# An expert layer over 63 tiles of gathered (token, expert) rows instead of 40 weight blocks over all tokens

## What is computed

```python
logits = x2d @ gate_w.T                                  # x2d: layer-normed tokens, 1024 x 256; 32 experts
rw = softmax(logits);  _, sel = top_k(sigmoid(logits), 4)
w = take_along_axis(rw, sel);  w = w / w.sum(-1)
cw_large = zeros(T, 32).at[rows, sel].add(w)             # 32 experts, 96 hidden units each
cw_small = zeros(T, 16).at[rows, sel // 2].add(w)        # 16 experts, 128 hidden units, one per pair of large ones
def moe(x, Wg, Wu, Wd, cw):
    a = silu(x @ Wg) * (x @ Wu) * cw
    return a @ Wd                                        # summed over the experts
x = x + moe(large) + 0.05 * moe(small)
```

## Time and profile before

| | us |
|---|---|
| median of three runs (lowest, highest) | 1066.67 (1061.46, 1066.79) |
| span of the profiled execution, first to last instruction | 1063.0 |
| of it: start, layernorm 1 and attention | 0 to 135 |
| `experts`, before its loop is in step | 135 to 162 |
| `experts`, the loop | 162 to about 488 |
| `experts`, the end | to 494.8 |
| `mamba` and `finish` | 494.8 to 1063 |

### The profile page before, as it was taken

How to read it: one execution, slowest core, us unless ns; L and a number is a source line. 1 busy time by engine, 2 the same in 40 slices (tenths; PEclk the granted TensorE clock), 3 DMA queues, 4 the chain that set the end, 5 groups by cost and what they waited for, 6 DMA issues and landing times. The chain is left out here.

```text
span 1063.0 us, 12994 instructions
## 1 busy us (share of the span) xinstructions
PE 946.7 (89%) x3808; PEld 594.9 (56%) x3808; DVE 852.0 (80%) x1118; ACT 563.1 (53%) x1130; POOL 691.1 (65%) x384
## 2 busy tenths in 40 slices
PE   5798879999999999996879897999989997877798
PEld 2466647888888888884434432443434342322587
DVE  3788777778778777776678989899988999999853
ACT  2688643333333333332777777775776667564141
POOL 3388625556555565562279998899989999999000
PEclk9999989999999999998989898899989998989899
DMA  3000036243342442413055575466655656554001
GB/s 95 1 2 0 1 124 170 84 139 105 103 138 84 123 138 69 124 54 93 15 151 146 155 185 159 125 162 172 156 136 146 162 152 160 154 167 119 0 1 41
DMA packets 59873, 114.53 MB, mean 108 GB/s; under 512 B 10368, under 2 KB 15744, under 8 KB 59696
## 3 DMA queue, kind: packets, MB, share of 16 engines
q1 hardware_dynamic: 58688, 112.08, 38.2%
q10 hardware_dynamic: 1136, 1.90, 0.5%
HBM read 112.45 MB, written 1.51 MB: 107 GB/s over the span
## 5 line engine op out<-in xcount | busy, mean ns | idle before, releaser
L1767 POOL TENSOR_TENSOR uB<-u,rows_B 128x1024 f32<-128x1024 f32 x127 | 299.1, 2367 | 0.5 <-DVE da L1984 0.5
L897 POOL TENSOR_TENSOR lutw<-lutw,lt 128x865 f32<-128x865 f32 x80 | 184.9, 2311 | 153.9 <-DVE lt L858 148.2
L2004 PE MATMUL ya<-hV,ident 128*128 128x512 f32 x320 | 180.5, 652 | 49.5 <-DVE hV L1884 40.2
L1984 DVE TENSOR_TENSOR_SCAN da<-da,uB 128x512 f32<-128x512 f32 x160 | 193.6, 1221 | 17.7 <-ACT da L1869 16.9
L1777 POOL TENSOR_TENSOR hP<-hS,rows_C 128x512 f32<-128x512 f32 x96 | 122.7, 1278 | 27.1 <-PE ya L2004 15.2
L2004 PEld LDWEIGHTS ya<-hV,ident 128*128 128x128 f32 x320 | 58.5, 200 | 140.6 <-DVE hV L1884 89.8
L1981 DVE TENSOR_TENSOR_SCAN hS<-da,uB 128x512 f32<-128x512 f32 x96 | 116.0, 1209 | 16.2 <-ACT da L1869 10.6
L759 ACT ACTIVATE ah<-ups 128x1024 fp32r<-128x1024 f32 x40 | 41.2, 1029 | 131.0 <-DVE ups L850 131.0
L1884 DVE TENSOR_TENSOR hV<-da,rows_C 128x512 f32<-128x512 f32 x160 | 106.8, 668 | 0.1
L2004 PE MATMUL ya<-hP,ident 128*128 128x512 f32 x192 | 102.0, 614 | 0.0
L847 DVE TENSOR_TENSOR si<-gps,cwb 128x1024 f32<-128x1024 f32 x40 | 49.0, 1224 | 52.9 <-ACT gps L756 52.9
(11 more groups left out here) (365 smaller groups left out, 2017.6 us busy)
## 6 DMA issues: line engine op xcount, KB each, us to landing
rows_B<-bc_rows SPq DMA_DIRECT2D x128, 256.0 KB, 3.7
rows_C<-bc_rows SPq DMA_DIRECT2D x128, 256.0 KB, 4.5
wr<-in_moe_w SPq DMA_DIRECT2D x40, 384.0 KB, 4.7
cwb<-cw_rows SPq DMA_DIRECT2D x16, 512.0 KB, 4.1
cwb<-cw_rows SPq DMA_DIRECT2D x15, 384.0 KB, 5.2
cwb<-cw_rows SPq DMA_DIRECT2D x16, 256.0 KB, 4.0
lut_f<-in_lut_idx SPq DMA_DIRECT2D x1, 2160.0 KB, 10.4
cwb<-cw_rows SPq DMA_DIRECT2D x15, 128.0 KB, 5.6
```

The costliest lines, as they stand in the source:

```text
L897: e.tensor_tensor(part, part, lt[:, q, :], ALU.add).then_inc(s_la, 1)
L1767: e.tensor_tensor(uB[:, r % UPAIRS, :, :], u[:, d:d + 2, :], RB[:, r % BROWS, :].unsqueeze(1).broadcast_to([P, 2, HALF]), ALU.mult).then_i ...
L1984: e.tensor_tensor_scan(a[:, way], a[:, way], uB[:, r % UPAIRS, b, way], 0.0, ALU.mult, ALU.add).then_inc(s_sc, 1)
L2004: return e.matmul(ya[n % 2][:, :], g.ident[:, :], at, start=False, stop=False, skip_group_check=True).then_inc(done, 1)
```

## The change

Instead of all blocks over all tokens, the (token, expert) pairs are sorted by expert on the chip into tiles of 128 pairs. Each of the 32 experts has one tile of its own; what an expert has beyond 128 pairs goes to overflow tiles, of which there are always 31, so 63 in all, whatever the routing. Free places point at 128 padding rows of zeros. In detail:

- **Lists.** After the router DVE makes a mask of the chosen experts, PE counts in nine float32 products how many tokens before each one chose the same expert (`tri`, `ones`), DVE turns the ranks into slots, then writes for each of 8 x 4 groups of pairs two one-hot matrices (`place_of`, `tile_of`), and PE multiplies them in 32 products into `li`, the list of rows for each tile. ACT writes normalised tokens and their weights to DRAM (`xs`, 1024 rows of 320 values).
- **Tiles.** For each tile POOL issues a gather of 128 rows (1280 bytes each), PE turns them (two transposes), computes gate and up of the large and small expert at once (two float32 products of 448 columns), turns the activations (two transposes) and computes the down product (two float32 products of 256 columns). ACT does silu and copies three results out of PSUM, DVE multiplies by up and by the row's weight (two instructions). POOL issues a scatter with addition of 128 rows of 1 KB to one of four tables `sums` in DRAM. For overflow tiles DVE picks the weight with two more instructions, and SP reads the expert's number from SBUF into a register to load its weights.
- **Weights.** 16 loads of 1 MiB for pairs of experts (`moe_two`), seven of them before the lists, five right behind them, four in the loop, then 31 loads of 704 KB (`moe_own`), in a ring of 12 places or 16. No splitting into high and low.
- **Table.** The 80 compares stay on DVE (16 of 16 values; the first goes straight to `lutw`), 60 of the adds move from POOL to DVE, 15 stay on POOL. 80 items are spread over the first 60 tiles.
- **End.** SP loads the four tables of sums (1 MiB each, after the last down product and the last scatter of each) and DVE adds each to `g.x` in one instruction of 128x2048.
- **Elsewhere.** SP fills the four tables and the padding rows with zeros during `attention` (five DMAs behind the later loads), and POOL sets a tile of zeros in `constants`.

The loops over tiles are written out, not rolled. The core of the diff (the lists and constants are left out):

```diff
+            def gather(t):
+                if t >= XG:
+                    e.wait_ge(s_tx, t - XG + 1)
+                    e.wait_ge(s_a, t - XG + 1)
+                e.indirect_dma_start(xg[:, t % XG, :], None, dram["xs"],
+                                     bass.IndirectOffsetOnAxis(ap=li[:, t:t + 1], axis=0)).then_inc(s_xg[t % XG], 16)
+            def scatter(t):
+                e.wait_ge(s_yc, t + 1)
+                if t >= NACC:
+                    e.wait_ge(s_sc[t % NACC], 16 * (t // NACC))
+                e.indirect_dma_start(dram["sums"][t % NACC], bass.IndirectOffsetOnAxis(ap=li[:, t:t + 1], axis=0),
+                                     y[:, t % NACC, :], None, compute_op=ALU.add).then_inc(s_sc[t % NACC], 16)
+            for s in range(TILES + 3):
+                if s + XG < TILES:
+                    gather(s + XG)
+                if 0 <= s - 3:
+                    scatter(s - 3)
+                for m in table_items(s):
+                    add(m)
```

with `XG` = 6 and `NACC` = 4, and on ACT:

```diff
+            def copy_y(t):
+                e.wait_ge(s_d, t + 1)
+                if t >= NACC:
+                    e.wait_ge(s_sc[t % NACC], 16 * (t // NACC))
+                e.activation(y[:, t % NACC, :], yps[:, t % 2, 0:D], ACT.Copy).then_inc(s_yc, 1)
+            for s in range(TILES + 2):
+                if s < TILES:
+                    silu(s)
+                if 0 <= s - 1 < TILES:
+                    copy_a(s - 1)
+                if s + 2 < TILES:
+                    copy_x(s + 2)
+                if 0 <= s - 2:
+                    copy_y(s - 2)
```

More of the change, by code:

```diff
@@ L663, in experts @@
[L663 to L676, removed]
+    taken = (PSLOTS - 5) * PAIR_W * 4
@@ L691, in _ @@
[L691 to L712, removed]
@@ L719, in _ @@
+            for i in range(TILES - NACC, TILES):
+                k = i % NACC
+                e.wait_ge(s_d, TILES)
+                e.wait_ge(s_sc[k], 16 * (i // NACC + 1))
+                e.dma_start(ysum[:, k, :, :], dram["sums"][k][0:T, :].rearrange("(n p) d -> p n d", p=P)
+                            ).then_inc(s_ld[k], 16)
         @block.scalar
         def _(e):
[L721 to L722 removed]
@@ new lines, in silu @@
+            def silu(t):
+                e.wait_ge(s_gu, t + 1)
+                if t >= 2:
+                    e.wait_ge(s_a, t - 1)
+                if second(t):
+                    e.activation(si[:, t % 2, INTER:], gups[:, t % 2, 0:CINTER], ACT.Silu)
+                    e.activation(si[:, t % 2, 0:INTER], gups[:, t % 2, BOTH - INTER:BOTH], ACT.Silu).then_inc(s_si, 1)
+                else:
+                    e.activation(si[:, t % 2, :], gups[:, t % 2, INTER:SHIFT + CINTER], ACT.Silu).then_inc(s_si, 1)
@@ L987, in _ @@
[L987 to L998 removed]
+            e.wait_ge(s_k1, 2)
@@ new lines, in gate_up @@
+            def gate_up(t):
+                e.wait_ge(s_xc, t + 1)
+                if t >= 2:
+                    e.wait_ge(s_a, t - 1)
+                    e.wait_ge(s_si, t - 1)
+                wait_weights(e, t)
+                both = weights(t)[0]
+                for k in range(KC):
+                    mm = e.matmul(gups[:, t % 2, 0:BOTH], xT[:, t % 2, k * P:(k + 1) * P], both[k], start=k == 0,
+                                  stop=k == KC - 1)
+                mm.then_inc(s_gu, 1)
@@ L1006 @@
+            e.wait_ge(s_li, 1)
+            turn_x(0)
+            turn_x(1)
+            e.wait_ge(s_wo, 2)
+            for s in range(TILES + 2):
+                if s < TILES:
+                    gate_up(s)
+                if 0 <= s - 1 < TILES:
+                    turn_a(s - 1)
+                if s + 2 < TILES:
+                    turn_x(s + 2)
+                if 0 <= s - 2:
+                    down(s - 2)
 NSEG = 4
```

628 lines of the change are left out of this document (385 added, 243 removed).

## The result

| | before | after |
|---|---|---|
| median (lowest, highest), us, 4 runs each | 1064.07 (1061.12, 1066.79) | 1021.39 (1018.85, 1026.25) |
| ratio, with 95% interval | | 0.9597 (0.9561 to 0.9634) |
| span of the profiled execution, us | 1063.0 | 1024.5 |

A forecast was written before the change was run, and what follows sets the result against it. PE bounded the old kernel; DVE, with PE close, would bound the new loop. Span: 135.1 + 45 (lists) + 204 (loop) + 20.4 (end) + 568.2 = 972.7 us, as a median 976; eight-in-ten range 950 to 1045.

The forecast's parts named there:

- What bounded the kernel before: In the old loop of the experts, PE is busy 320.3 of 324 us, so only less PE work or another bound changes it.
- Attention, +2.3 us: Stage before the experts: 135.1 us, unchanged, with SP's five zero fills hidden, or 2.3 us at the most.
- Lists, +3.7 us: From the end of attention to the first gate-and-up product: 45 us, bounds 41 to 52.
- the landing: Behind `li`, POOL's first gather lands in 3 us, after an issue of 1.3.
- The loop, +42.9 us: The loop of 63 tiles takes 204 us, bounds 190 to 236.
- the price of an issue: POOL's time per gather or scatter in the loop: 1.3 us, between 0.46 and 2.31; POOL needs 199 us in all.
- DVE sets the pace: In the loop DVE is longest: 2.95 us per tile for the first 32 tiles, 3.45 for the others, 201 us.
- The rival: In the loop POOL becomes the bound: at 1.7 us an issue, 1024 us; chance 0.26, shared with POOL and DVE excluding each other.
- The exclusion: In the loop POOL's issues and DVE's compares cannot overlap: loop 260, time 1032 us; chance 0.26, shared with POOL as bound.
- the free price of the add: DVE's table add without POOL at work: 1.05 us, against 1.9 with it; at this price the loop is 190 us.
- DMA: right: DMA needs 167 us and fits under the loop's 204; as the bound it gives a loop of 223, 995 us; chance 0.06.
- The end, +2.7 us: From the last down product to the next stage: 20.4 us, 19 of it for four loads and the last add.

## Why the prediction was half right

**What bounded the kernel before: right.** Less work on PE made the kernel faster, and its work per tile was near the forecast: with no DMA on POOL it is busy for 178.7 us of 190, about 2.9 us per tile for the 2.79 of the sum.

**Attention, +2.3 us: not the zero fills.** The version with plain scatters has no fill of the four tables (the DMA share from 20 to 60 us is 0.11, in the change 0.37) and still ends attention at 137.49. The kernel with the adds on DVE has all fills and ends it at 134.81. What goes with the end is the granted clock from 20 to 60 us: 1.00 in the kernel before and in the one that ended at 134.81, 0.94 in one that ended at 135.31, 0.90 to 0.91 in the nine that ended at 136.15 to 137.75. Why it differs between executions stays open.

**Lists, +3.7 us: the working held, the landing did not.** From the end of attention to `li` it was 39.5 us (forecast 37.9). Behind it:

```profile
176.61 0.28 DVE L935 TENSOR_SCALAR li<-yps,lastrow 128x64 int32<-128x64 f32 x1 [1.22 <-PE yps L1135]
177.20 1.18 POOL L1067 DMA_INDIRECT xg<-x_rows,li  x1 [26.09 <-DVE li L935]
...
184.67 0.66 PE L1144 MATMUL xps<-ident,xg 128*128 128x128 f32 x2 [8.09 <-DMA xg<-x_rows,li]
```

The first gather took 7.5 us from the start of its issue to the turn; I had 4.3, from the earlier trace rows. SP starts five loads of 1 MiB on the same signal; that these delay it is argued, not tried. In the other kernels with the same lists the whole term took 45.1 to 48.6 us. (PE's counting is ten products, not the nine named; their 1408 columns are right. The recorded steps add up to 177.9 and not to 178.5.)

**The loop, +42.9 us: POOL's issue.** The step that failed is the price of an issue, "I take 1.3, the row of POOL's instruction with 512 columns", and with it that DVE sets the pace. Two things were off. The issues themselves measured 1.170 and 1.792, a mean of 1.48: 22.8 us more over 126. And the sum had no gap between two instructions of POOL: 37 us. Together 1.78 us per issue, well above the 1.34 "up to which nothing changes". From the forecast's 199 us for POOL: 22.8 for the issues, 3.8 for dearer adds, 37 for the gaps and 7 for waits, less the 8 in which adds and issues overlap, give the measured chain of 261.6.

The rival was there and priced: POOL as the bound at 1.7 us gives 1024, and the time is 1021. The mechanism is right, the nearness is luck: at the measured 1.78 the same formula gives a loop of 262 us, 15 more than measured, as it counts the gathers ahead of the loop, the scatters behind it and no overlap. At 1.7 its loop was 5 us too long; the other terms of the span were 9 too short and the step to the median 7 too long, and so 3 us are left. The rival got too small a chance, because the price was chosen for want of a nearer row, and the choice of 1.3 put it just under DVE; with bounds of 0.46 and 2.31 about as much of the interval lies above 1.34 as below. The exclusion was no pure case either: it came on top.

**DVE: its work too high, PE's too low.** Per tile I had 2.95 and 3.45 us for DVE with the add at 1.35. With no DMA on POOL a tile takes 2.87 and 3.07, and it is PE that is full in the first half, not DVE: 193.6 us in all, near the 190 that the forecast had for the free price of the add, where "PE takes over in the first half". So the 204 was 10 us too high, and in the change neither engine set the pace (DVE at 71% and 84% of two stretches, where above 90% was the sign). The add costs 1.05 where POOL does no adds, 1.19 in the change; the compare, which I took at 0.725 throughout, costs 1.006 there for 0.751. So POOL's adds cost the 75 compares about 19 us and the 60 adds 8.5: the slowing was put on the instruction that bears less of it. The timeline shows a case of it, an instruction of DVE beside an add of POOL (the row of POOL is above, at 310.64):

```profile
310.45 3.25 DVE L1003 TENSOR_SCALAR lt<-lut_f,iota_l,lutb 128x865 f32<-128x865 f32 x1
```

Alone it takes 0.72 us; here it ends 0.5 us after POOL's 2.59. The Trainium skill (SBUF — State Buffer, Who interferes with whom) says that this is a lock held for a whole instruction and that it holds up GpSimd's DMA issues as well. On the first the trace agrees that the one ends only after the other; it does not show who has the lock, as the compare's record starts 0.19 us ahead of the add's and it is the compare that is held. On the second it shows 24 us of 187, a lengthening by 0.17 to 0.21 us of an issue on average, and a maximum of 2.87 us for one of 1.56; the full exclusion that I priced as a rival (a loop of 260) did not come.

**DMA: right.** Its share is 0.77 in the loop, and no run points to it as the limit: with the gathers as plain loads the share is 0.94 from 184 to 278 us, with both as plain DMAs 0.81, and the loop is the same.

**The end, +2.7 us.** Four loads, then one add each:

```profile
435.47 9.60 SPq L771 DMA_DIRECT2D ysum<-y_sums  x4
441.86 2.29 DVE L1034 TENSOR_TENSOR x<-x,ysum 128x2048 f32<-128x2048 f32 x1 [10.12 <-DMA ysum<-y_sums]
...
452.08 2.29 DVE L1034 TENSOR_TENSOR x<-x,ysum 128x2048 f32<-128x2048 f32 x1 [0.63 <-DMA ysum<-y_sums]
```

The first load starts 2.5 us behind the last down product, since SP waits for the landing of the fourth scatter from the end, whose issue ran until 433.17 us; the three behind it stand in POOL's queue until 438.77. The rest is as forecast, the add at 2.29 for 2.3.

## What to carry to other kernels

An engine that is busy with each DMA that it issues has a price list: count its issues, add the gap behind each, and look at start-to-start steps and not at the busy share, because 81% busy can be full. A wait "for a DMA" may be a wait for its issue: measure from the moment the data was ready to the start of the issue before more buffers are given to it. And where a price has no row, and the break-even lies inside its bounds, the two sides get chances by the width of the interval and not by the value that was taken.

## What the runs showed of the hardware

- An indirect DMA of 128 rows keeps GpSimd busy for 0.94 us (gather of 1280-byte rows) or 0.97 us (scatter of 1 KB rows) at the shortest, 1.56 us if the scatter adds; 0.30 us pass between two of them. 64 rows fewer in an adding scatter save 0.17 us.
- An add in DRAM is thus paid at the issue, 0.60 us of GpSimd's time, not only by the DMA engines.
- A compare of 865 columns on VectorE beside a two-operand add on GpSimd takes 3.25 us for 0.72; the add of two SBUF operands on VectorE takes up to 3.9 us for 1.05. With all adds on VectorE the longest compare is 0.98 us and the longest add 1.06.
- Granted clock from 20 to 60 us of attention, whose work is the same in all kernels but for the zero fills: 1.00, 0.94 or about 0.91 in the twelve executions traced; the stage ends 1 to 3 us later where it is lower.
